# Three small products joined in one in a chunked delta-rule kernel

## What is computed

```python
def step(S, inp):
    qt, kt, vt, gt, bt = inp
    S = S * jnp.exp(gt)[..., None, None]
    pred = jnp.einsum('bhk,bhkv->bhv', kt, S)
    dv = (vt - pred) * bt[..., None]
    S = S + jnp.einsum('bhk,bhv->bhkv', kt, dv)
    ot = jnp.einsum('bhk,bhkv->bhv', qt, S)
    return (S, ot)
...
o = o * jax.lax.rsqrt(jnp.mean(o * o, -1, keepdims=True) + 1e-05) * norm_w
o = o * jax.nn.silu(gate)
return o.reshape(Bh, Tt, Hh) @ Wo.T
```

## Time and profile before

| | |
|---|---|
| median of 3 runs | 1757.93 us |
| runs | 1755.05, 1757.93, 1771.21 us |
| span of the profiled execution | 1760.8 us |
| busy: TensorE, its weight loads | 1679.1 us (95%), 1411.3 us (80%) |
| busy: VectorE, ScalarE, GpSimd | 1263.6 (72%), 1203.0 (68%), 461.1 us (26%) |
| mean granted clock of TensorE | 0.968 |

### The profile page before, as it was taken

One profiled execution on the slowest core, in us unless ns is written; L12 is line 12 of the kernel. 1 busy time (PEld: TensorE's weight loads), 2 busy tenths in 40 slices (PEclk: granted clock), 3 DMA queues, 4 the chain that ended last, 5 costly groups with the idle time before them and its releaser, 6 DMA issues.

```text
span 1760.8 us, 108854 instructions
## 1 busy us (share of the span) xinstructions
PE 1679.1 (95%) x49152; PEld 1411.3 (80%) x49152; DVE 1263.6 (72%) x3718; ACT 1203.0 (68%) x2241; POOL 461.1 (26%) x389
## 2 busy tenths in 40 slices
PE   5699999999999999999999999999999999999886
PEld 4487888888888888888888888888888888887775
DVE  4866777887767788777778777777877777887441
ACT  7666776677677667777766777676676767667445
POOL 0223332223333222333322233322223332222301
PEclk9889999999999999999999999999999999999876
DMA  3000000000000000000000000000000000000000
GB/s 121 1 4 4 5 16 16 16 16 16 10 10 16 16 16 16 16 4 16 16 16 16 16 16 4 16 17 16 16 16 16 4 16 10 10 10 10 10 10 13
DMA packets 21614, 26.95 MB, mean 15 GB/s; under 512 B 2208, under 2 KB 20768, under 8 KB 21152
## 3 DMA queue, kind: packets, MB, share of 16 engines
q1 hardware_dynamic: 21152, 19.99, 3.5%
HBM read 11.60 MB, written 8.39 MB: 11 GB/s over the span
## 4 chain that ended last, share of the span: by engine, by line
PE 88%; issue 6%; DVE 4%; ACT 2%; POOL 1%; ACTq 0%; DVEq 0%; POOLq 0%
PE ps L242 40%; PE ps L224 15%; PE ps L233 10%; PE ps L217 7%; PE ps L443 3%; PE ps L210 3%; PE ps L394 2%; PE ps L347 2%; PE ps L532 2%; PE ps L538 2%; PE ps L362 1%; DVE CV L1071 1%; ACT L621 0%; ACT L618 0%; DVE TZ L1093 0%
## 5 line engine op out<-in xcount | busy, mean ns | idle before, releaser
L1071 DVE SCALAR_TENSOR_TENSOR CV<-ps,cw,CV 128x256 f32<-128x256 f32 x576 | 233.9, 475 | 49.4 <-ACT CV L664 48.9
L242 PEld LDWEIGHTS ps<-MQ,S 64*64 64x64 f32 x4096 | 145.3, 139 | 60.3 <-issue 45.9
L1178 DVE TENSOR_TENSOR MQ<-GQ,ps 128x384 f32<-128x384 f32 x32 | 17.7, 554 | 227.9 <-PE ps L242 227.9
L242 PE MATMUL ps<-MQ,S 64*64 64x16 f32 x4096 | 170.6, 212 | 1.8 <-ACT S L615 1.8
L986 POOL TENSOR_TENSOR ST<-GB,msk 128x512 f32<-128x512 f32 x32 | 41.6, 1300 | 469.1 <-ACT GB L883 469.1
L951 POOL TENSOR_TENSOR XK<-XK 128x512 f32<-128x512 f32 x32 | 33.3, 1040 | 470.2 <-ACT XK L705 470.2
L615 ACT ACTIVATE S<-SA,pair 128x512 f32<-128x512 f32 x128 | 81.9, 710 | 96.5 <-DVE SA L1103 96.5
L242 PEld LDWEIGHTS ps<-VT,WP 32*32 32x32 f32 x8192 | 89.5, 108 | 70.1 <-issue 58.0
L618 ACT ACT_TABLE_LOAD x112 | 143.7, 1283 | 2.5 <-DVE prod L1411 0.6
L621 ACT ACT_TABLE_LOAD x111 | 142.4, 1283 | 1.9
L217 PE MATMUL ps<-XK,w_k_ffn 128*128 128x256 f32 x512 | 136.6, 413 | 4.9 <-DVE XK L1058 4.8
(11 more groups left out here) (138 smaller groups left out, 3878.7 us busy)
## 6 DMA issues: line engine op xcount, KB each, us to landing
X<-in_x SPq DMA_DIRECT2D x32, 256.0 KB, 2.8
out_x<-X SPq DMA_DIRECT2D x32, 256.0 KB, 2.3
KQI<-in_blocks SPq DMA_DIRECT2D x2, 256.0 KB, 4.2
w_r_ffn<-in_wT_r_ffn SPq DMA_DIRECT2D x1, 256.0 KB, 3.3
w_k_ffn<-in_wT_k_ffn SPq DMA_DIRECT2D x1, 256.0 KB, 3.5
w_v_ffn<-in_wT_v_ffn SPq DMA_DIRECT2D x1, 256.0 KB, 5.3
w_k<-in_wT_k SPq DMA_DIRECT2D x1, 256.0 KB, 4.4
w_q<-in_wT_q SPq DMA_DIRECT2D x1, 256.0 KB, 4.7
```

What stands on the lines that cost most here:

```text
L242: last = mm(ps[rows, o:o + n], stat[rows, pk].rearrange("p s c -> p (s c)"), mov[rows], **flags)
L1071: stt(d4[:, m], src, cw[:, i, m, tap:tap + 1], d4[:, m], ALU.mult, ALU.add).then_inc(signal, 1)
```

## The change

For each chunk, pack and pair of heads one 32 x 32 product now gives the state after the chunk and the chunk's output at once. The moving operand MV holds, for one head of a pair, 16 rows of state and 16 rows of v; the stationary Z2 holds in its four 16 x 16 parts the map of state to state, state to output, v to state and v to output. `b_product` and `o_product` go, with ScalarE's `s_slots` and `v_slots`, and with V2, S4, VT, SA and one of the two WP. `chain` issues, per chunk, 4 packs x 2 heads of a pair x 4 row quarters = 32 products (before: 16 of `b_product` and 16 of `chain`). `d_product` has 64 columns in place of 48, `d_out` 512 in place of 384, adding. On VectorE the copy of the state becomes a predicated copy of four times 32 columns under a mask of rows (`copy_predicated`), out of half a PSUM bank of which the other 16 rows are outputs; every second chunk `o_turn` turns 256 columns of that bank into OB; `o_merge` puts the two heads of a pair together after ScalarE's `o_first` has copied one of them. `o_square` and `o_norm` read the result OM in SBUF. The copy of `chain` 7 moves on VectorE from behind `d_out0` to behind the second `solve_sub`. GpSimd gets `q_slots` (1024 columns), `k_beside` (2048 columns, adds identity blocks into spare slots of KD4) and `v_both` (512 columns). The tile pair, loaded once, is 100 columns wider. VectorE keeps all its other segments in their order.

```diff
             def d_product0(g):
                 pe.wait_ge(s["wp"], 2 * g + 1)
-                pe.wait_ge(s["gram_used"], 4 * g + 4)
+                pe.wait_ge(s["kdi"], g + 1)
...
-                    last = pairs(PS["d0"] * BANK + i * 3 * C, 3 * C, KD4, pk, WP[g % 2][:, pk], start=True, stop=True)
+                    last = pairs(PS["d0"] * BANK + i * 2 * U, 2 * U, KD4, pk, WP[:, pk], start=True, stop=True)
...
             def wo(g):
                 pe.wait_ge(s["ot"], g + 1)
-                pe.wait_ge(s["osq"], g + 1)
+                if g >= 2:
+                    pe.wait_ge(s["x3"], g - 1)
...
             def chain(g, n):
                 if n == 0:
                     pe.wait_ge(s["mt"], 4 * g + 4)
-                pe.wait_ge(s["ch_s"], NCH * g + n)
-                m2 = MQ[g % 2][:, :, 0:U].rearrange("p k (s c) -> p k s c", s=2)
+                    pe.wait_ge(s["v2"], g + 1)
+                pe.wait_ge(s["ch_s"], NCH * g + n + 1)
+                if g or n >= 2:
+                    pe.wait_ge(s["ob"], 4 * g + n // 2)
                 for ub in range(M * B):
                     pk = ub * NCH + n
-                    last = pairs(PS["b"] * BANK + (n * M * B + ub) * D, D, m2, pk, SA[g % 2][:, pk * D:(pk + 1) * D],
-                                 start=False, stop=True, skip_group_check=True)
+                    for ab in range(2):
+                        o = PS["ch"] * BANK + n % 4 * M * B * U + (ub * 2 + ab) * C
+                        for q in range(P // U):
+                            rows = slice(q * U, (q + 1) * U)
+                            last = mm(ps[rows, o:o + C], Z2[g % 2][rows, pk, ab * U:(ab + 1) * U], MV[g % 2][rows, pk, ab, :],
+                                      start=True, stop=True)
                 last.then_inc(s["ch_ps"], 1)
...
-                for h in range(2):
-                    own.done(af(WP[g % 2][:, rows, h * C:(h + 1) * C], src[:, :, C:U], ACT.Copy, scale=slot[:, h:h + 1]))
-                nc.scalar.copy(WP[g % 2][:, rows, U:], src[:, :, 0:C]).then_inc(s["wp"], 1)
+                src = bank(PS["t0"])
+                own.done(af(WP[:, rows, 0:U], vw(src[:, C:], [U, C], [-C, 2], [1, C]), ACT.Copy, scale=slot[:, 0:1]))
+                af(WP[:, rows, U:], src.rearrange("p (k c) -> p k c", c=U), ACT.Copy, scale=slot[:, 1:2]).then_inc(s["wp"], 1)
...
+            def o_first(g):
+                act.wait_ge(s["ob"], 4 * g + 4)
+                if g:
+                    act.wait_ge(s["ot"], g)
+                af(packs(OM[:]), OB[:, :, C:], ACT.Copy, scale=slot[:, 0:1]).then_inc(s["om_first"], 1)
...
+            def q_slots(g):
+                pool.wait_ge(s["qe"], g + 1)
...
+            def k_beside(g):
+                pool.wait_ge(s["gram_used"], 4 * g + 4)
+                dst = KD4[:].rearrange("p k s c -> p k (s c)")
+                tt(dst, dst, over_packs(beside4), ALU.add).then_inc(s["kdi"], 1)
+
+            def v_both(g):
+                pool.wait_ge(s["vt"], g + 1)
+                nc.gpsimd.tensor_copy(MV[g % 2][:, :, 1, :], MV[g % 2][:, :, 0, :]).then_inc(s["v2"], 1)
...
             def chain(g, n):
                 ve.wait_ge(s["ch_ps"], NCH * g + n + 1)
...
-                nc.vector.tensor_copy(vw(dst[:, m * D:], [TG, M * B], [1, D]), vw(src, [D, M * B], [1, D])).then_inc(s["ch_s"], 1)
+                nc.vector.copy_predicated(state_rows_of(dst, m), vw(state_rows, [0, M * B], [1, U]),
+                                          vw(src, [U, M * B], [1, U])).then_inc(s["ch_s"], 1)
+
+            def o_turn(g, t):
+                ve.wait_ge(s["ch_ps"], NCH * g + 2 * t + 2)
...
+                nc.vector.transpose(vw(OB[:, 2 * t], [U, 2], [NCH * U, M * B], [1, U]),
+                                    vw(src, [M * B * U, 2], [U, M * B], [1, U])).then_inc(s["ob"], 1)
+
+            def o_merge(g):
+                ve.wait_ge(s["om_first"], g + 1)
+                ve.wait_ge(s["ob"], 4 * g + 4)
+                stt(packs(OM[:]), OB[:, :, 0:C], slot[:, 1:2], packs(OM[:]), ALU.mult, ALU.add).then_inc(s["om"], 1)
...
-                tt(MQ[g % 2][:, rows], GQ[:, rows], src, ALU.subtract).then_inc(s["mt"], 1)
+                src = bank(PS["d0"]).rearrange("p (k c) -> p k c", c=2 * U)
+                tt(Z2[g % 2][:, rows], GZ[:, rows], src, ALU.add).then_inc(s["mt"], 1)
...
                 on(chain, step - 4, 5)
+                on(o_turn, step - 4, 2)
                 on(conv_v, step - 2)
                 on(solve_mul, step - 3, 1)
                 on(chain, step - 4, 6)
                 on(solve_sub, step - 3, 1)
                 on(solve_mul, step - 3, 2)
                 on(solve_sub, step - 3, 2)
+                on(chain, step - 4, 7)
+                on(o_turn, step - 4, 3)
...
                 on(stats2, step - 1)
+                on(o_merge, step - 4)
...
                 on(d_out0, step - 3)
                 on(shift1, step)
-                on(chain, step - 4, 7)
                 on(d_out1, step - 3)
...
                 on(chain, step - 3, 1)
+                on(o_turn, step - 3, 0)
...
                 on(chain, step - 3, 3)
+                on(o_turn, step - 3, 1)
```

More of the change, by code:

```diff
@@ L27 @@
 CT = KC - 1
-NX, NGS, NVT = 8, 4, 3
+NX, NGS = 8, 4
 RING = 8
@@ L78, in macaron_kernel @@
         KQI = [sb(f"KQI{i}", [P, 3, COLS]) for i in range(2)]
-        VT = [sb(f"VT{i}", [P, COLS]) for i in range(NVT)]
+        MV = [sb(f"MV{i}", [P, PACKS, 2, C]) for i in range(2)]
+        none = sb("none", [P, U])
         E = sb("E", [P, COLS])
@@ L91, in macaron_kernel @@
         T2 = sb("T2", [P, PACKS, 2, C])
[L92 to L95, removed]
+        K4, KD4 = (sb(n, [P, PACKS, HT, C]) for n in ("K4", "KD4"))
+        WP = sb("WP", [P, PACKS, 2 * U])
+        OB = sb("OB", [P, PACKS, U])
+        OM = sb("OM", [P, COLS])
         OSQ = sb("OSQ", [P, COLS])
@@ L491, in ffn3_r @@
                 rows_out(PS["r3"], w["r_ffn"], XR[1], s["r3_ps"])
-            def o_product(g, h):
-                if h == 0:
-                    pe.wait_ge(s["s_slots"], 4 * g + 4)
-                    pe.wait_ge(s["v_slots"], 2 * g + 2)
-                    pe.wait_ge(s["mt"], 4 * g + 4)
-                if h == 0:
-                    if g >= 2:
-                        pe.wait_ge(s["x3"], g - 1)
-                part = range(h * PACKS // 8, (h + 1) * PACKS // 8)
-                for pk in part:
-                    pairs(PS["o"] * BANK + pk * C, C, S4, pk, MQ[g % 2][:, pk, U:], start=(pk == 0), stop=False,
-                          skip_group_check=True)
-                for pk in part:
-                    last = pairs(PS["o"] * BANK + pk * C, C, V2, pk, WP[g % 2][:, pk, U:], start=False, stop=True,
-                                 skip_group_check=True)
-                last.then_inc(s["o_ps"], 1)
             def v_proj(g):
@@ L559, in _ @@
                 on(k_proj, step - 1)
-                on(b_product, step - 3, 0)
                 on(chain, step - 3, 0)
@@ L564, in _ @@
                 on(q_proj, step - 1)
-                on(b_product, step - 3, 1)
                 on(chain, step - 3, 1)
@@ L859, in t_out1 @@
-                for h in range(2):
-                    own.done(af(WP[g % 2][:, rows, h * C:(h + 1) * C], src[:, :, C:U], ACT.Copy, scale=slot[:, h:h + 1]))
-                nc.scalar.copy(WP[g % 2][:, rows, U:], src[:, :, 0:C]).then_inc(s["wp"], 1)
+                src = bank(PS["t1"])
+                own.done(af(WP[:, rows, 0:U], vw(src[:, C:], [U, C], [-C, 2], [1, C]), ACT.Copy, scale=slot[:, 0:1]))
+                af(WP[:, rows, U:], src.rearrange("p (k c) -> p k c", c=U), ACT.Copy, scale=slot[:, 1:2]).then_inc(s["wp"], 1)
@@ L922, in _ @@
                 on(tap_v, step - 1)
-                on(v_slots, step - 3)
                 on(halo3, step - 4)
                 on(relu1, step)
-                on(s_slots, step - 3)
                 on(xt3, step - 4)
@@ L932, in _ @@
                 on(square_k, step - 1)
+                on(o_first, step - 3)
                 ln_exp_set()
@@ L1021, in _ @@
                 on(q_decayed, step - 1)
+                on(q_slots, step - 1)
                 on(square3, step - 4)
                 on(e_mask, step - 1)
+                on(v_both, step - 1)
+                on(k_beside, step - 1)
         @block.vector
@@ L1406, in _ @@
             own.done(nc.vector.memset(Y3[:, :, TG:], 0.0))
-            own.done(nc.vector.memset(SA[0][:], 0.0))
+            own.done(nc.vector.memset(none[:], 0.0))
             own.settle()
```

148 lines of the change are left out of this document (61 added, 87 removed).

## The result

The changed kernel takes 2034.87 us (median of 4 runs, 2026.98 to 2035.84) against 1762.34 us for the kernel before: a ratio of 1.1543, 95% interval 1.1495 to 1.1591. The sign is that of the prediction; the size (+272 us in place of +100) is outside its range. The profiled execution has a span of 2032.2 us.

What follows compares the result with a forecast made beforehand. The prediction took a closed ring of VectorE then TensorE as the bound: 51.91 - 1.03 + 2.10 + 0.20 = 53.2 us a round, 55.6 with half clock; +111 - 11 us in all gave 1858 us, range 1780 to 1930.

Steps and rivals of the forecast that it cites:

- That hides them: GpSimd's added `q_slots`, `k_beside` and `v_both` cost nothing, since GpSimd waited 14.7 us a round for `square1`'s input.
- The 0.72 us wait for `chain` 5 disappears: VectorE comes later to `chain` 5, so its wait goes, leaving net 2.10 us of added VectorE time a round.
- The ring: VectorE's 41.24 us from `d_out0` through `t_turn`, then TensorE's 9.64 us; removing TensorE work saves only 1.03 us a round.
- TensorE's own work: Falls by `o_product`'s 7.52 us to 44.4 us a round; joined `chain` and 64 column `d_product` add nothing.
- VectorE's additions: Predicated copies 0.44, copy of `chain` 7 0.28, `o_turn` 1.41, `o_merge` 0.69 us: sum 2.82 us a round.
- The clock: TensorE idles some 6 us ahead of `t_product`, then runs at half clock: 2.4 us lost a round.
- The 0.2 for ScalarE: Copying the T product's second half, ahead of `d_product2`, adds 0 to 0.47 us a round; 0.2 taken.
- the last rounds and the drain: At the end, the last group's `o_product` stands bare; its removal saves 11 us.
- The clock did not hold: Rival: TensorE's gap breaks into small ones and the clock holds; 53.2 us a round, 1785 us; chance 17%.
- TensorE's stream did not set the round: Rival: TensorE's stream alone sets the round, which falls to 44.4 us; 1522 us; chance 5%.
- The dear case: Rival: two-pass copies, dear turns, `d_product` by columns, half clock for 7.5 us; 60.5 us a round, 2005 us; 11%.

Runs made afterwards that it cites:

- a_parts: The changed kernel with GpSimd's `k_beside` split into four adds of 512 columns, each issued as soon as its gram is done: 1932.87 us, ratio 1.0914.
- a_clear: a_parts with GpSimd's order also changed to `square3`, `e_mask`, the four `k_beside`, `v_both`, `q_slots`: 1888.69 us, ratio 1.0664.
- b_no_o2: The kernel before without `o_product`'s products, each of its eight parts replaced by one 128x128 product of 64 columns: 1744.08 us, ratio 0.9867.
- a_off: a_clear with two VectorE instructions moved: `solve_sub` 0 behind `conv_v`, `o_merge` behind `t_turn`: 1841.62 us, ratio 1.0407.
- a_best: a_off plus ten unread TensorE products ahead of `t_product` 0, and the copy of `chain` 7 and `o_turn` 3 moved behind `t_turn`: 1765.45 us, ratio 0.9965.
- a_fill: a_clear plus twelve TensorE products of 256 columns, whose result nobody reads, just ahead of `t_product` 0: 1834.18 us, ratio 1.0369.
- b_add_solve: The kernel before plus one scratch GpSimd add of 2048 columns a round, released after `solve_sub` 3 within the solve: 1901.20 us, ratio 1.0775.

## Why the prediction was wrong

**The step that failed is "That hides them", on GpSimd.** The prediction sized `k_beside` rightly (3.9 us; 3.81) and asked who waits in GpSimd's own queue behind it, where the earlier trace rows show ample room. It did not ask what VectorE does beside it; that VectorE's operations keep their length it said of TensorE only. VectorE's stretch is 8.2 - 2.1 = 6.1 us over the forecast: 2.45 us `solve_mul` 0, 1.68 us `mix_k1`, 2.00 us the wait for `chain` 5 that follows from the first and 0.40 us one for `chain` 7 (the rest of the stretch is 0.4 us under). The runs price it: a_parts takes 102 us off and a_clear another 44, of the 177 us between forecast and result; by the ratios, which take out the difference between chips, 6.3% and 2.5% of the kernel before.

The Trainium skill, "SBUF — State Buffer", section "Who interferes with whom", states the rule: a VectorE instruction with two SBUF inputs contends with a GpSimd instruction that reads SBUF, one with at most one SBUF input doesn't (outside certain modes), and the ports that the two engines share are an exclusive lock. The runs agree: in three kernels the held instruction ended 0.04 us after GpSimd's, and `a_turn`, with one such input, took 1.06 us beside `k_beside` and 1.03 without it. In the kernel before, `gram3` ends at 940.91 and `solve_mul` 0 starts at 942.15 (rows above). By the rule, an estimate: the 3.9 us of `k_beside` would have held it 2.7 us a round, some 80 us. The trace of the kernel before shows such a hold too, once, while the pipeline fills, VectorE's second instruction of `g_reduce` and then GpSimd's `g_ident`:

```profile
54.47 1.87 DVE L1280 TENSOR_TENSOR eg<-eg,pair 128x128 f32<-128x128 f32 x1
```
```profile
54.23 1.96 POOL L947 TENSOR_TENSOR GQ<-pair,EQ 128x1024 f32<-128x1024 f32 x1
```

In its other 31 groups that instruction takes 0.29 us.

**"The 0.72 us wait for `chain` 5 disappears" failed with it**: it became 2.00 us, because TensorE stood idle behind the late copy of `chain` 3 and resumed at half clock. Nor was there that much to gain: the round that was read had a long wait, and the mean over the 32 groups is 0.31 us. In a_clear the wait ahead of `chain` 5 is nearly gone (0.11 us on the mean), but the copy of `chain` 7 waits in its new place, 0.45 us in the round shown and 0.74 on the mean.

**Right, by its own steps.** *The ring*: b_no_o2 removes the work and adds nothing, and of 6.0 us none comes back in the middle rounds; the moves off the ring in a_off and a_best return what the ring theory says (47 us, expected 49; and, against a_fill, 69 us, expected 70). *TensorE's own work*: the 64 column product takes 4.11 us against 3.98. *VectorE's additions*: from start to start in a_clear, a copy takes 0.20 us (0.13 before, being lengths), an `o_turn` 0.37, `o_merge` 0.66: 7 x 0.07 + 0.20 + 1.48 + 0.66 = 2.83 us, forecast 2.82. *The clock*: 11.99 us for TensorE's part, forecast 9.64 + 2.4 + 0.2. The 0.2 for ScalarE is not to be seen: at full clock a_fill has 9.52 us.

**Off in size**: the last rounds and the drain. Head and tail together (the span less the 31 rounds) lose 4.5 us, not 11. And the cleared kernel is 31 us over the forecast, 12 of which are its chip, where the kernel before took 1770 us. That its round comes so near the forecast's 55.6 us is in part luck. Its middle rounds are 4.9 us longer than before (forecast 3.7). VectorE's stretch is 3.9 us longer, forecast 2.1: `solve_mul` 0, `solve_sub` 0 and the first instruction of `mix_k1` are still held beside GpSimd's `v_both`, `square1` and `e_mask`, 1.2 us by their means, and the waits for `chain` did not go. TensorE's part is 1.0 us longer, forecast 1.6: there the low clock costs 2.0 us (11.65 against a_fill's 9.61) where the sum had 2.4.

**The rivals.** The clock did not hold, and TensorE's stream did not set the round. The dear case came near the number for none of its reasons: no copy took two passes and no turn the dear pace.

## What to carry to other kernels

An engine with time to spare is free only for work that holds up nothing beside it. Before moving work to GpSimd, lay its instructions beside VectorE's timeline, and let each VectorE instruction there that reads two operands from SBUF wait until GpSimd's has ended. Put long GpSimd work beside VectorE's work on PSUM, or cut it so that no piece is running when the two-operand stretch begins. And where a ring over two engines is closed, taking work off the fuller engine pays nothing until the ring is shorter, and may cost its clock: look for the place where the other engine waits anyway and move the additions there. A hold in that place is free as well: in the changed kernel `k_normed`, behind `t_turn`, takes 1.47 us in place of 0.74, and VectorE still waits 9 us for TensorE behind it.

## What the runs showed of the hardware

A 30 column VectorE instruction of 0.20 us took 3.37 us beside one GpSimd add, and ended 0.04 us after it. One instruction is held, not each a little: behind the 4.57 us of b_add_solve's `soft_part` the solve goes on at its old lengths. The profile counts the hold as busy time of VectorE, not as a wait; what gives it away is an end that follows closely on that of a GpSimd instruction. It goes both ways to some degree: in the changed kernel GpSimd's `square3` and `e_mask` beside `mix_k1` took 1.55 and 1.44 us, against 1.04 and 1.27 us in a_clear. The 2048 column copy took 1.89 us where the add took 4.52. And fillers that TensorE runs for nobody are worth 54 us here, because the products that follow them are on the path.
